# Graph attention and a routed FFN on one core: row fetches with a bound, and source numbers past it for rows of other destination blocks

## The chip, the cores and the metric

The kernel runs as one program on one core of a Trainium2 chip. The metric is the device time of one execution in microseconds (us); the figure given for a kernel is the median of its runs. The profile comes from one further execution; it counts times from the start of its own span. Engine names: PE is the matrix engine, PEld its weight load, DVE the vector engine, ACT the scalar engine, POOL the GpSimd engine, SP the engine that only issues DMAs. An engine's name with a q behind it (POOLq) is its instruction queue, that is, instructions which the sequencer carries out by itself.

## What is computed

There are 2500 nodes with 256 features and 80000 edges (`src`, `dst`), sorted by `dst`. The first half of the layer is a graph attention with 4 heads of 64 features; the second half is a feed-forward layer with 8 experts, of which each node takes two.

```python
h = einsum('nf,hfo->nho', layernorm(x), W)
e_s = einsum('nho,ho->nh', h, a_src)
e_d = einsum('nho,ho->nh', h, a_dst)
scores = leaky_relu(e_s[src] + e_d[dst], 0.2)
m = segment_max(scores, dst)
ex = exp(scores - m[dst])
alpha = ex / maximum(segment_sum(ex, dst)[dst], 1e-9)
agg = segment_sum(alpha[:, :, None] * h[src], dst)
x = x + relu(agg)
x = x + ffn(layernorm(x))    # 8 experts, top 2, HID = 512
```

## The kernel before

**Stages.** The program has three stages one after the other. The setup normalises `x`, multiplies it with the weights and stores one row per node in a DRAM table `h_tab` (2560 rows of 260 fp32: 256 of h, then e_s of the 4 heads). The edge loop fetches one such row per edge and sums them by destination. The last stage is the routed FFN.

**Tiles.** The nodes are cut into 20 blocks of 128 destinations (NB), the edges into 625 chunks of 128 (CHUNKS). A tile is one chunk seen by one block: where a block begins in the middle of a chunk, that chunk is in two tiles, once for either block. Each block has an even number of tiles, so some have a tile more than they need, and the program is built for the most that can be needed, NT = 664 tiles. For each tile a column of `srcP` holds the source numbers of its 128 edges, and a column of `Dcol` their destination less 128 times the block. An edge whose destination is in the block has a number from 0 to 127 there. Any other edge has one outside, its row of the one-hot matrix `dst_oh` is zero, and the row that was fetched for it adds nothing.

**Layout of the tiles.** DVE finds the counts (L985 to L1021). POOL fetches the chunks' edges by indirect DMA (L507) into `lay`; DVE makes `D_f` from the destinations (L1076), copies the sources to floats `s_f` (L1078), makes the marks between segments `RS_rows` (L1079 to L1082) and some flags, and tells the others by `lay_ready` (L1092). Then it zeroes `acc` (L1094). PE turns `D_f` and `s_f` (L604, first piece at the seventh of ten projections, which are L592), ACT copies them to `Dcol` and `srcP` (L793 to L800) and one small turned piece to `row_src` (L817), for which DVE waits at L1101.

**Edge loop.** It goes in phases of 32 tiles (PH) and in batches of 8 (BT). Whose turn it is:

- POOL issues one indirect DMA a tile (L529), 128 rows of 1040 bytes into the slot t mod 128 of `ring`. From tile 80 on (AHEAD) each eighth one waits until PE has done the batch 80 tiles back.
- DVE waits until a phase's 32 tiles have landed (`weights`, first instruction L1140), works out the maxima of the segments by scans, and multiplies the rows by the weights batch by batch (`weigh`, L1205, L1206). It adds PE's sums to `acc` (`flush`, L1118).
- ACT makes the one-hot matrices (L826, L831). PE multiplies them with the rows (`batch`, L641 to L643), two tiles to one sum.

**Order of the queues.** Each engine's order is written out by hand. Ahead of the first L529, POOL's queue holds 21 fetches of destinations (L496, L501), 6 of chunks (L507) and 20 scatters (L516), and waits for the stored `h_tab` and for the layout (L519 to L525). Behind the last one stand the FFN's gathers and scatters (L540, L549).

Of the kernel before, what the change touches and what calls it, by code (L numbers as in the profile page):

```python
# [37 lines left out]
def gat_moe_kernel(nc, x, src, dst, gnn_w, a_src, a_dst, gamma, beta, wr, br, w1, b1, w2, b2, out):  # L38
    fp32, bf16, i32 = mybir.dt.float32, mybir.dt.bfloat16, mybir.dt.int32
    ALU = mybir.AluOpType  # L40
    ACT = mybir.ActivationFunctionType
    AX = mybir.AxisListType
    P = 128

    N, F = x.shape
    H, _, FO = gnn_w.shape
    HF = H * FO
    KF = F // P
# [5 lines left out]
    NB = (N + P - 1) // P  # L55
# [6 lines left out]
    TG = (NPH * PH + P - 1) // P  # L62
# [9 lines left out]
    assert NT % BT == 0 and CHUNKS * P == E and RING % PH == 0 and H * PH == P  # L72
    MW = HF + H
    NE, _, HID = w1.shape
    FC = HID // P
    BS = 256
# [2 lines left out]
    NBLK = (TOP * N + NE * (BS - 1)) // BS  # L79
    EG = (N + BS - 1) // BS  # L80
    BIG = 1e38
    EPS = 1e-5

    h_tab = nc.dram_tensor("h_tab", (NB * P, MW), fp32).ap()
# [13 lines left out]
    with ctx:  # L98
        def sb(name, shape, dt=fp32):
            return ctx.enter_context(nc.sbuf_tensor(name, shape, dt))  # L100
# [12 lines left out]
        def early(width, dt=fp32):  # L113

            a = ring_flat[:, used[0]:used[0] + width]
            used[0] += width
            return a if dt == fp32 else a.bitcast(dt)
# [17 lines left out]
        D_f, s_f = (early(TG * P).rearrange("p (g e) -> p g e", g=TG) for _ in range(2))  # L135
        RS_rows = early(TG * P).rearrange("p (g e) -> p g e", g=TG)
# [23 lines left out]
        srcP = sb("srcP", [P, NPH * PH], i32)  # L160
# [320 lines left out]
        def _(pool):  # L481
# [8 lines left out]
            for t, pattern, mult in ((iota_f, [[1, P]], 0), (pcol, [[1, 1]], 1), (p128, [[1, 1]], P),  # L490
# [7 lines left out]
                in_offset=bass.IndirectOffsetOnAxis(ap=qbi[:, 0:1], axis=0)).then_inc(brow_in, 16)  # L498
            pool.wait_ge(q_ready, 1)
            for b in range(NB):  # L500
                pool.indirect_dma_start(  # L501
                    out=drow[:, b, :], out_offset=None, in_=dst_rows,
                    in_offset=bass.IndirectOffsetOnAxis(ap=qi[:, b:b + 1], axis=0)).then_inc(rows_got[b], 16)
            pool.wait_ge(chunks_ready, 1)
            pool.wait_ge(ds_put, 32)
            for g in range(TG):
                pool.indirect_dma_start(  # L507
                    out=lay[:, g, :], out_offset=None, in_=ds_tab,
                    in_offset=bass.IndirectOffsetOnAxis(ap=chunk_i[:, g:g + 1], axis=0)).then_inc(lay_in, 16)
# [16 lines left out]
            for t in range(NT):  # L526
                if t % BT == 0 and t >= AHEAD:
                    pool.wait_ge(batch_done, (t - AHEAD) // BT + 1)
                pool.indirect_dma_start(  # L529
                    out=ring[:, t % RING, :], out_offset=None, in_=h_tab,  # L530
                    in_offset=bass.IndirectOffsetOnAxis(ap=srcP[:, t:t + 1], axis=0))\
                    .then_inc(gathered[t // PH % len(gathered)], 16)

# [31 lines left out]
        def _(pe):  # L566
# [101 lines left out]
            def nodes_T(i):  # L668
                pe.wait_ge(x1_made, 1 + sum(2 * i + 2 > hi for _, hi in SETS))
                if i >= 2:  # L670
                    pe.wait_ge(xT1_copied, i - 1)
                for b in range(2):
                    for k in range(KF):
                        last = pe.transpose(bank[i % 2][:, (k * 2 + b) * P:(k * 2 + b + 1) * P],  # L674
                                            acc[:, 2 * i + b, k * P:(k + 1) * P], ident[:, :])
                last.then_inc(xT1_done, 1)
# [278 lines left out]
        def _(v):  # L955
            c = Chain(v, s_dve)
            v.memset(xs0[:, NB - 1, :], 0.0).then_inc(pads_set, 1)
            v.memset(bigs, -BIG).then_inc(bigs_set, 1)
            for t in (part_ends, C):
                v.memset(t[:, :], 0.0)  # L960
            v.memset(A_row[:, 0:1], -BIG)
            v.memset(D_row[:, P:P + 1], -BIG)
            v.memset(RS_all[:, :, P:P + 1], -BIG)
            v.wait_ge(ends_in, 16)
# [60 lines left out]
            def x_stats(lo, hi):  # L1025
# [9 lines left out]
                c.link(v.scalar_tensor_tensor(sm1[:, of], sm1[:, of], F / 4.0, sm2[:, of], ALU.mult, ALU.add))  # L1035
                v.tensor_scalar(sm1[:, of], sm1[:, of], 1.0 / F, EPS, ALU.mult, ALU.add).then_inc(var_ready, 1)

# [38 lines left out]
                last = v.tensor_scalar(D_f[:, g, :], lay_d[:, g, :], d_sub[:, g:g + 1], None, ALU.subtract)  # L1076
            c.link(last)
            v.tensor_copy(s_f, lay_s)  # L1078
            c.link(v.tensor_tensor(RS_rows[:, :, 1:P], D_f[:, :, 0:P - 1], D_f[:, :, 1:P], ALU.is_equal))  # L1079
            c.link(v.tensor_scalar(RS_rows[:, :, 1:P], RS_rows[:, :, 1:P], 1.0, BIG, ALU.subtract, ALU.mult))  # L1080

            v.memset(RS_rows[:, :, 0:P:PH], -BIG)  # L1082
            parts_of = D_f.rearrange("p g (i r) -> p g i r", r=PH)
# [192 lines left out]
            def stats(n):  # L1276
# [3 lines left out]
                for b in range(lo, hi):  # L1280
# [10 lines left out]

                v.tensor_scalar(tmp1[:, of], tmp1[:, of], (1.0 + EPS) / F, EPS * EPS, ALU.mult, ALU.add)\
                 .then_inc(var_ready, 1)
# [212 lines left out]
```

## Time and profile before

| | |
|---|---|
| time, median of 3 runs | 1388.14 us |
| lowest and highest of them | 1386.94 and 1390.61 us |
| span of the profiled execution | 1249.1 us |
| that execution's own time | not recorded beside its profile |
| first L529 starts, last L529 starts | 78.6 us, 910.4 us |
| POOL busy | 784.9 us (63%) |
| DVE busy | 726.1 us (58%) |
| PE busy | 661.5 us (53%) |
| ACT busy | 419.7 us (34%) |

The span begins with the first instruction and ends with the last. 1388.14 - 1249.1 = 139.0 us of a run's time lie around it, and no view shows them. POOL's busy time in a DMA row is the time in which it writes descriptors; the data move afterwards.

### The profile page before, as it was taken

The page shows a single profiled execution, that of the slowest core. Times are in us where ns is not written, and L with a number is a line of the kernel's source. Part 1 is how long each engine was busy: PE and PEld are TensorE (multiplying, and loading weights), DVE is VectorE, ACT ScalarE, POOL GpSimd, SP SyncE. Part 2 cuts the span into 40 slices and gives each one's busy share as a digit, 9 for nine tenths or more (in the row PEclk, how much of TensorE's full clock was granted, in tenths as well). Part 3 has the DMA queues.
Part 4 walks back from the last instruction along what each step waited for, and adds up shares of the span by engine and source line. Part 5 has one row for each costly group of instructions (what it writes and reads, how often), then busy time and mean ns, then how long its engine had stood idle before and what let it go on. Part 6 is the DMA issues. An engine that isn't in the chain of part 4 may idle for free.

```text
span 1249.1 us, 11021 instructions
## 1 busy us (share of the span) xinstructions
PE 661.5 (53%) x2666; PEld 524.6 (42%) x2666; DVE 726.1 (58%) x1781; ACT 419.7 (34%) x1058; POOL 784.9 (63%) x835
## 2 busy tenths in 40 slices
PE   0630343455335643465435643365447579999990
PEld 0520232244223432344324432244336558888880
DVE  6611476558665775558655775558677853333325
ACT  3550243144323443144423443144421532222210
POOL 5577777777777777777777777777710025555540
PEclk9975657787678766777677776776777579999995
DMA  8564434344444434444344444443491212222217
GB/s 281 177 119 108 110 106 109 109 111 110 107 110 110 110 107 108 109 111 110 107 111 110 111 107 109 109 111 106 118 357 44 84 34 69 76 72 72 68 59 254
DMA packets 79451, 143.95 MB, mean 115 GB/s; under 512 B 22337, under 2 KB 50467, under 8 KB 79267
## 3 DMA queue, kind: packets, MB, share of 16 engines
q0 software_dynamic: 39664, 110.31, 31.9%
q1 hardware_dynamic: 37147, 30.44, 8.0%
q10 hardware_dynamic: 2584, 2.56, 0.6%
q8 instruction: 22, 0.36, 0.1%
q14 instruction: 34, 0.28, 0.1%
HBM read 126.48 MB, written 17.40 MB: 115 GB/s over the span
## 4 chain that ended last, share of the span: by engine, by line
POOL 50%; PE 19%; issue 18%; DVE 6%; DMA 2%; PEld 1%; ACT 1%; PEldq 1%; DVEq 0%; POOLq 0%
POOL ring L529 49%; PE psum L731 7%; PE psum L745 7%; PE psum L592 1%; POOL ring L501 1%; PEld psum L641 1%; PEldq L643 1%; PE psum L719 1%; PE psum L683 1%; DVE acc L1479 1%; DVE acc L1480 1%; ACT ring L882 1%; PE psum L674 1%; DMA ring<-in_dst,ring 1%; DMA h_tab<-ring 1%
## 5 line engine op out<-in xcount | busy, mean ns | idle before, releaser
L529 POOL DMA_INDIRECT ring<-h_tab,srcP x664 | 630.8, 950 | 204.6 <-issue 201.9
L641 PE MATMUL psum<-ring,shared 128*128 128x260 f32 x1328 | 387.0, 448 | 450.5 <-DVE acc L1118 391.9
L641 PEld LDWEIGHTS psum<-ring,shared 128*128 128x128 f32 x1328 | 284.1, 222 | 540.2 <-DVE acc L1118 407.4
L826 ACT ACTIVATE shared<-iota_f,Dcol 128x128 f32<-128x128 f32 x664 | 202.0, 386 | 29.6 <-PEq L643 29.5
L1205 DVE TENSOR_TENSOR ring<-ring,psum 128x2048 f32<-128x2048 f32 x83 | 189.8, 2287 | 2.8
L844 ACT ACTIVATE Ex<-Z 128x128 f32<-128x128 f32 x21 | 6.5, 309 | 516.8 <-DVE Z L1172 516.8
L1118 DVE TENSOR_TENSOR acc<-acc,psum 128x260 f32 x332 | 140.0, 422 | 59.7 <-PEq L643 24.2
L1140 DVE STREAM_TRANSPOSE TB<-ring 128x128 f32<-128x128 f32 x21 | 8.5, 403 | 226.4 <-DMA ring<-h_tab,srcP 226.3
L540 POOL DMA_INDIRECT ring<-z_tab,ring x54 | 52.5, 972 | 116.4 <-DVEq L1418 100.3
L549 POOL DMA_INDIRECT ys_tab<-shared,ring x54 | 53.9, 998 | 85.5 <-DVE shared L1438 77.2
L928 ACT ACTIVATE RS_all<-psum,tail_consts 128x256 f32<-128x256 f32 x108 | 45.2, 470 | 158.0 <-PE psum L731 158.0
L745 PE MATMUL psum<-ring,RS_all 128*128 x432 | 97.5, 379 | 0.0
L731 PE MATMUL psum<-ring 128*128 128x256 f32 x432 | 97.5, 379 | 0.0
L831 ACT ACTIVATE shared<-shared,ones 128x1024 f32<-128x1024 f32 x83 | 95.3, 1149 | 2.7
L731 PEld LDWEIGHTS psum<-ring 128*128 128x128 f32 x432 | 82.0, 190 | 11.1
L745 PEld LDWEIGHTS psum<-ring,RS_all 128*128 128x128 f32 x432 | 80.1, 190 | 9.9
L1438 DVE TENSOR_TENSOR shared<-psum,links 128x512 f32<-128x512 f32 x27 | 18.7, 691 | 74.2 <-PE psum L745 74.2
L1430 DVE TENSOR_SCALAR ring<-psum,tail_consts 128x256 f32<-128x256 f32 x54 | 26.8, 538 | 53.0 <-PE psum L719 53.0
L516 POOL DMA_INDIRECT ed_tab<-e_node,spos x20 | 19.8, 991 | 12.9 <-ACT e_node L808 8.0
L1422 DVE COPY ring<-ring 128x1024 f32 x27 | 19.3, 713 | 14.0 <-issue 10.7
L501 POOL DMA_INDIRECT ring<-in_dst,ring x20 | 18.9, 946 | 10.5 <-issue 5.8
L592 PE MATMUL psum<-ring 128*128 128x264 f32 x80 | 20.3, 398 | 0.0
(293 smaller groups left out, 620.5 us busy)
## 6 DMA issues: line engine op xcount, KB each, us to landing
ring<-h_tab,srcP POOLq DMA_INDIRECT x664, 2.8
ring<-in_L_ffn_W SPq DMA_DIRECT2D x16, 512.0 KB, 11.0
h_tab<-ring SPq DMA_DIRECT2D x10, 260.0 KB, 2.6
ring<-in_x SPq DMA_DIRECT2D x1, 2432.0 KB
z_tab<-ring SPq DMA_DIRECT2D x2, 1024.0 KB, 4.4
ring<-ys_tab SPq DMA_DIRECT2D x4, 512.0 KB, 9.0
ring<-ys_tab ACTq DMA_DIRECT2D x4, 512.0 KB, 9.6
out<-acc SPq DMA_DIRECT2D x4, 512.0 KB
```

Of the source, the lines that this page charges most:

```text
L529: pool.indirect_dma_start(out=ring[:, t % RING, :], out_offset=None, in_=h_tab, in_offset=bass.IndirectOffsetOnAxis(ap=srcP[:, t:t + 1], a ...
L540: pool.indirect_dma_start(out=xs_in[:, u, m, :], out_offset=None, in_=z_tab, in_offset=bass.IndirectOffsetOnAxis(ap=node_ix[:, BM * j + m: ...
L549: pool.indirect_dma_start(out=ys_tab, out_offset=bass.IndirectOffsetOnAxis(ap=dest_ix[:, BM * j + m:BM * j + m + 1], axis=0), in_=y_out[:, ...
L592: last = pe.matmul(bank[2 + 2 * (i % 2) + b][:, 0:wide], xT0[:, i % 2, b, k, :], w_ext[:, k, :], start=(k == 0), stop=(k == KF - 1))
L641: pe.matmul(sums[G_at % NSUM][:, 0:MW], dst_oh[:, n % OHB, 2 * g + r, :], ring[:, t % RING, :], start=(r == 0), stop=(r == 1))
L731: last = pe.matmul(bank[2 + 2 * u + c // 2][:, c % 2 * BS:(c % 2 + 1) * BS], w1_now[:, u, k, c * P:(c + 1) * P], xsT[:, u, k, :], start=(k ...
L745: last = pe.matmul(bank[6 + u][:, m * F:(m + 1) * F], hT[:, u, c, m * P:(m + 1) * P], w2_all[:, bass.ds(e, 1), c, :].rearrange("p e f -> p ...
L826: last = act.activation(dst_oh[:, n % OHB, k, :], iota_f[:, :], ACT.Square, scale=-1.0, bias=Dcol[:, t:t + 1])
L831: act.activation(batch, batch, ACT.Relu, scale=-1.0, bias=ones[:, 0:1]).then_inc(oh_made, 1)
L928: act.activation(hT[:, u, c, :], bank[2 + 2 * u + c // 2][:, c % 2 * BS:(c % 2 + 1) * BS], ACT.Gelu, bias=b1_T[:, bass.ds(e * FC + c, 1)]) ...
L1118: v.tensor_tensor(a, a, sums[(n * GB + g) % NSUM][:, 0:MW], ALU.add).then_inc(flushed, 1)
L1205: v.tensor_tensor(msg, msg, ex.unsqueeze(3).broadcast_to([P, BT, H, FO]), ALU.mult)
```

## The change

A constant `FAR` (8192) is added. After the floats of the sources have been made, three DVE instructions on columns 1 to 5 of the six columns of tiles (each column has 128 tiles, so on tiles 128 to 767) work out D (D - 127), which is above 0 just where D is outside 0 to 127, make 8192 or 0 of it, and add that to the source number. They use `RS_rows`, which is written right after them, as their scratch. Each of the 664 fetches now has a bound, 2559, the last row of `h_tab`, and the mark that an index past the bound is no error: nothing is fetched for it. The slots of tiles from 128 on then keep the rows of the tile 128 before; the first 128 tiles fetch all their rows, since their slots hold something else before.

```diff
+    FAR = 8192
...
                 pool.indirect_dma_start(
                     out=ring[:, t % RING, :], out_offset=None, in_=h_tab,
-                    in_offset=bass.IndirectOffsetOnAxis(ap=srcP[:, t:t + 1], axis=0))\
+                    in_offset=bass.IndirectOffsetOnAxis(ap=srcP[:, t:t + 1], axis=0),
+                    bounds_check=NB * P - 1, oob_is_err=False)\
                     .then_inc(gathered[t // PH % len(gathered)], 16)
...
             v.tensor_copy(s_f, lay_s)
+            away = RS_rows[:, 1:TG, :]
+            far_of = D_f[:, 1:TG, :]
+            c.link(v.scalar_tensor_tensor(away, far_of, 1.0 - P, far_of, ALU.add, ALU.mult))
+            c.link(v.tensor_scalar(away, away, 0.5, float(FAR), ALU.is_gt, ALU.mult))
+            c.link(v.tensor_tensor(s_f[:, 1:TG, :], s_f[:, 1:TG, :], away, ALU.add))
             c.link(v.tensor_tensor(RS_rows[:, :, 1:P], D_f[:, :, 0:P - 1], D_f[:, :, 1:P], ALU.is_equal))
```

The order of DVE in the setup, before (all of these names lie in the buffer `ring`, which the setup uses as its scratch):

```order
L1076 TENSOR_SCALAR ring<-ring 128x128 x6
L1078 CAST ring<-ring 128x768
L1079 TENSOR_TENSOR ring<-ring 128x6x127
L1080 TENSOR_SCALAR ring<-ring 128x6x127
L1082 MEMSET ring 128x24
```

The same place with the change, where each line number is 2 to 7 higher:

```order
L1078 TENSOR_SCALAR ring<-ring 128x128 x6
L1080 CAST ring<-ring 128x768
L1083 SCALAR_TENSOR_TENSOR ring<-ring 128x640
L1084 TENSOR_SCALAR ring<-ring 128x640
L1085 TENSOR_TENSOR ring<-ring 128x640
L1086 TENSOR_TENSOR ring<-ring 128x6x127
```

Three instructions of 640 elements a partition have come in between the cast and the marks; nothing else has changed places on DVE, PE, ACT or SP. On POOL the 664 fetches stand where they stood.
How many rows are skipped follows from the inputs: 4352 of the 68608 rows of tiles 128 to 663 (6.3%). They are in 50 tiles, mostly in twos and threes at the border of two blocks; 18 tiles are skipped whole. Nine of these are the last nine, 655 to 663.

## Rows read from the trace of the kernel before

**Rows 1.** Busy time by stage: setup, edge loop, FFN (columns in the first line)
```profile
core 0: us, PE busy (x) PEld busy (x) DVE busy (x) ACT busy (x) POOL busy (x), PEclk, DMA share, GB/s
0.00:78.60 78.60, 28.32 (x145) 23.99 (x145) 43.79 (x139) 34.08 (x79) 47.71 (x63) 0.98 0.71 207
78.60:911.40 832.80, 371.96 (x1289) 275.14 (x1290) 520.34 (x1288) 303.91 (x791) 630.81 (x664) 0.71 0.41 111
911.40:1249.00 337.60, 261.18 (x1233) 225.46 (x1232) 161.96 (x355) 81.71 (x188) 106.41 (x108) 0.84 0.32 104
```

**Rows 2.** Groups of POOL: busy us, mean ns | idle before, releaser
```profile
L529 POOL DMA_INDIRECT ring<-h_tab,srcP x664 | 630.8, 950 | 204.6 <-issue 201.9 <-DMA h_tab<-ring 2.6
L549 POOL DMA_INDIRECT ys_tab<-shared,ring x54 | 53.9, 998 | 85.5 <-DVE shared L1438 77.2 <-issue 8.2
```

**Rows 3.** Line L529: duration in ns, least, median, most; who waited for it
```profile
L529 POOL DMA_INDIRECT ring<-h_tab,srcP x664: 942/946/1133, 78.6 to 910.4; - x166
...
  DVE TB L1140: 226.3, 20
...
DMA to landing us min/median/max: 2.7/2.8/3.9
```

**Rows 4.** Timeline around the end of the edge loop: POOL, then DVE
```profile
910.42 0.94 POOL L529 DMA_INDIRECT ring<-h_tab,srcP  x1 [0.30 <-issue]
...
924.72 0.40 DVE L1140 STREAM_TRANSPOSE TB<-ring 128x128 f32<-128x128 f32 x1
```

**Rows 5.** Other indirect DMAs, by line, as in Rows 3
```profile
L501 POOL DMA_INDIRECT ring<-in_dst,ring x20: 942/946/955, 11.1 to 34.8; - x20
...
L516 POOL DMA_INDIRECT ed_tab<-e_node,spos x20: 954/958/1148, 50.3 to 75.0; - x20
```

**Rows 6.** POOL's queue, lines L487, L505 and L523, as in Rows 3
```profile
L487 POOLq MOVE  x3: 29/29/35, 1.3 to 1.5; - x3
...
L505 POOLq EVENT_SEMAPHORE  x1: 17/17/17, 20.8 to 20.8; - x1
...
L523 POOLq EVENT_SEMAPHORE  x1: 43/43/43, 70.9 to 70.9; - x1
```

**Rows 7.** Timeline of POOL: start, us, what [idle before, releaser]
```profile
34.82 0.95 POOL L501 DMA_INDIRECT ring<-in_dst,ring  x1 [0.30 <-issue]
36.07 0.95 POOL L507 DMA_INDIRECT ring<-ds_tab,ring  x1 [0.30 <-issue]
...
53.17 1.15 POOL L516 DMA_INDIRECT ed_tab<-e_node,spos  x1 [0.30 <-issue]
54.62 1.15 POOL L516 DMA_INDIRECT ed_tab<-e_node,spos  x1 [0.30 <-issue]
56.07 0.96 POOL L516 DMA_INDIRECT ed_tab<-e_node,spos  x1 [0.30 <-issue]
...
75.01 0.95 POOL L516 DMA_INDIRECT ed_tab<-e_node,spos  x1 [0.31 <-issue]
78.60 0.99 POOL L529 DMA_INDIRECT ring<-h_tab,srcP  x1 [2.64 <-DMA h_tab<-ring]
```

**Rows 8.** Timeline of DVE in the setup
```profile
53.40 0.95 DVE L1079 TENSOR_TENSOR ring<-ring 128x762 f32<-128x762 f32 x1
54.38 0.56 DVE L1080 TENSOR_SCALAR ring<-ring 128x762 f32<-128x762 f32 x1
...
55.43 0.31 DVE L1091 COPY ring<-ring 128x6 f32<-128x6 f32 x1
...
64.68 0.17 DVE L1101 TENSOR_TENSOR ring<-psum,ring 128x6 f32<-128x6 f32 x1 [2.86 <-ACT ring L817]
```

**Rows 9.** Timeline of PE in the setup
```profile
62.46 0.60 PE L604 MATMUL psum<-ident,ring 128*128 128x128 f32 x4
```

**Rows 10.** DMA queue of POOL: packets, MB, share of 16 engines
```profile
q0 software_dynamic: 39664, 110.31, 31.9%
```

## Prediction

> **What bounds the kernel now.** I cut the span into its stages first [rows 1]: 78.6 us of setup, 832.8 us of edge loop, 337.6 us of FFN. In the edge loop no engine is busy all the time by that view; POOL has the most, 630.8 us of 832.8, and the DMA engines only 0.41 of theirs. The groups of POOL then show what fills the rest [rows 2]: 664 fetches of 950 ns on average and 201.9 us of idle time put down to "issue", which is time in which POOL waited for nobody. That is 201.9 / 663 = 0.305 us behind each. So POOL takes 950 + 305 = 1255 ns a tile without a break, and 664 x 1.255 = 833 us is the whole stage. The line's own view confirms it from the other side [rows 3]: the fetches are as good as equally long (median 946 ns), the wait for a batch that each eighth one carries has never held one up, and DVE waited 20 times, 226.3 us in all, for a phase to land. Everybody waits for POOL's descriptor writing. It is neither bytes nor DMA engines. A step in the edge loop is therefore worth what it does to those 1255 ns, and nothing else.
>
> One exception is at the end. The 21st phase starts on DVE at 924.72, and it did not wait for the fetches: the last had been issued at 910.42 + 0.94 and needs 2.8 us to land, so it was there at 914.2, 10.5 us early [rows 3, 4]. Phase 21 has the tiles 640 to 663. What changes in these 24 fetches is hidden by 10.5 us; what changes in the 640 before moves the end.
>
> **The change, part by part.**
>
> *Three DVE instructions in the setup.* The nearest rows have 762 elements and take 0.95 us (two inputs) and 0.56 us (one input) [rows 8]. For 640 elements that gives 0.80 + 0.47 + 0.80 = 2.1 us, between the cast and `lay_ready`, which comes at 55.7 now. Three wait behind them. PE's first turning of the layout starts at 62.46 [rows 9], 6.7 us after `lay_ready`, so it stays. DVE's L1101 waits 2.86 us for ACT [rows 8], which leaves 0.8. POOL's scatters beside DVE's work took 1.15 us and alone 0.96 [rows 7], so some two more scatters lie beside it and cost 2 x 0.19 = 0.4 us; the last of them ends at 75.96 and the first fetch waits until 78.60 for the stored table, so that is hidden by 2 us. All of it costs nothing. If the covers were gone it would be 2.1 us, once.
>
> *664 register moves.* A move on POOL's queue took 29 ns [rows 6]. One end of its price is that all is in series: 29 ns each, and 640 x 29 = 19 us. The other end is nothing, and three things speak for it. The wait of L505 stands behind the twentieth L501, which started at 34.82, yet it ran at 20.8, a dozen fetches ahead, and the gap at its place between L501 and L507 is 0.30 like every other [rows 6, 7]. L523 stands behind the last scatter (75.01) and ran at 70.9 [rows 6, 7]. The sequencer thus runs at least four DMAs ahead of the descriptor writing, and has 1255 ns per tile for a move of 29. I take nothing.
>
> *The bound in the fetch.* This is what decides, and the trace shows no fetch with a bound. The bounds of its price come from the other forms of the same instruction, all with 128 indices. L501 takes 946 ns at the median for rows of 2560 bytes, as L529 does for 1040, so bytes are free; L516, which writes by an index instead of reading by one, takes 958 [rows 3, 5]. The dearest form, L549, has a mean of 998, 48 ns above L529's 950 [rows 2]. A bound means that someone compares 128 numbers and treats some as absent, in every one of the 664, skipped rows or not. I take the step between the two nearest forms, 958 - 946 = 12 ns: 640 x 12 = 7.7 us. The ends are 0 and 640 x 48 = 31 us. Below nothing it can only come by what is skipped.
>
> *4352 rows less.* The DMA engines are at 0.41 and nobody waits for one for want of bandwidth [rows 1], so 6.3% fewer bytes bring nothing by themselves. A skipped row brings time only if POOL saves the writing of its descriptor. Split evenly, a row is worth at most 946 / 128 = 7.4 ns. Of the 4352 rows 9 x 128 = 1152 are in the covered phase 21, so at most 3200 x 7.4 = 24 us are there to have. The lower end is 0. I take 0, since that an instruction takes 942 to 946 ns whatever it moves [rows 3, 5] looks more like a fixed course than like work by the row; but all forms have 128 indices, so it does not exclude the other. The Trainium skill (DMA: Bandwidth & Descriptors, Anatomy of one DMA) calls descriptor generation "small, variable" and says that many descriptors can be emitted before the incremental cost shows. By that the saving would be 0 too, and a fetch here should be short; the row of 946 ns, which is not small, does not bear the first half out [rows 3].
>
> Sum: 0 + 0 + 7.7 - 0 = +7.7 us. The profiled execution's span becomes 1249.1 + 7.7 = 1256.8 us. With the 139.0 us around the span, which the change does not touch, the time is **1395.8 us**, 1388.14 + 7.7. The 139.0 come from the runs' median, as the profiled execution's own time is not given.
>
> **The rivals.** A measurement of this kernel can tell about 0.3% from no change, that is 4.2 us, or 6.5 ns on each of the 640 fetches. That is little.
>
> *A. Nothing happens.* The comparison fits into the fixed course, the moves hide: 1388 us. For it: 942, 946 and again 946 ns in quite different gathers [rows 3, 5]. Against it: a scatter, which differs by as little, is 12 ns longer.
>
> *B. Faster: skipped rows are not written.* It decides if POOL's time goes by the descriptors written and the test is cheap. With all of 7.4 ns a row it is -24 us, 1364 us; with half of it and no price for the test, 1376 us. It would need a saving of more than 12 x 640 / 3200 = 2.4 ns a skipped row to outweigh the price that I took. Against it: 4352 rows are few beside 664 instructions, so a price per instruction weighs 640 times and the saving sits in 41 tiles (the 50 less nine).
>
> *C. The moves are in series.* If a fetch that reads a register holds the queue until the one before is done, each tile has 29 ns more: +19 us, and with the forecast's 12 ns +26 us, 1414 us. Against it are the rows on L505 and L523; for it only that neither of them feeds the DMA behind it.
>
> *D. The test is made index by index.* Then it lengthens the writing by a share of 946 ns. A tenth gives 640 x 0.095 = 61 us and 1449 us, and there is no clear upper end. Against it: nothing in the rows shows a loop by the index. The Trainium skill (GPSIMD Engine Reference, Elementwise — side-by-side cycle accounting) states that data-dependent branching costs about 12 cycles an element on this engine; 128 of them at its 1.2 GHz would be an estimated 1.28 us a fetch and over 800 us in all, which would more than double the stage. No run here shows a branch by the element.
>
> **How the numbers follow.** Forecast (a few to 48 ns on each fetch, +4 to +31 us): 0.36. A, same: 0.34. B, faster: 0.17. C: 0.06. D: 0.07. So faster 0.17, same 0.34, slower 0.36 + 0.06 + 0.07 = 0.49. Cases of both signs have their part, but the forecast's own range is 1392 to 1419. The range for all goes down to 1368, which takes in most of B (its last 4 us need the full 7.4 ns a row), and up to 1425, which takes in the upper end of the forecast and C, and leaves out D. Some 0.07 + 0.04 + 0.03 are outside.
>
> **What would show it.** The fetch's own line shows nearly everything. Forecast: its median is 955 to 960 ns instead of 946, and the same in tiles with and without skipped rows, the gap behind it still 0.30, and the moves stand in POOL's queue well ahead of their fetches. A: median 946. B: the fetches of the 18 whole tiles, in pairs with their neighbours, are clearly shorter than 942, which now is the least. C: gaps of 0.33 or more. D: median above 1.0 us. In all cases the first fetch stays at 78.6 and `lay_ready` comes 2.1 us later; the bytes of the software queue fall by 4352 x 1040 = 4.5 MB from 110.31 [rows 10]. The prediction is wrong if the first fetch moves, if DVE no longer waits at L1140 (then another engine sets the pace, for which nothing speaks with DVE busy 520 of 833 us [rows 1]), or if fetches begin to wait for a batch.

## The result and the profile after

| | before | changed |
|---|---|---|
| median, lowest and highest of 4 runs | 1388.91 (1386.94 to 1390.61) us | 1397.30 (1395.32 to 1401.98) us |
| the profiled execution's own time | not recorded | 1395.32 us |
| its span | 1249.1 us | 1393.5 us |

The ratio is 1.0072, with a 95% interval of 1.0056 to 1.0088. The change costs 0.7%; the forecast was 1395.8 us.

The table's last two lines already break one step of the working. In the changed kernel the span falls short of the execution's time by 1.8 us, not by 139. No 139 us lie around a span. The profile of before was of another kind of execution than the runs beside it; with some 2 us around its span it took about 1251 us in all, an inference that the repeated runs below bear out. How that can be comes out in the experiments: **the same program took about 1390 us in the runs on some chips and about 1250 us in those on others.**

The stages of the changed kernel, in its own profile, to be held against [rows 1]:

```profile
core 0: us, PE busy (x) PEld busy (x) DVE busy (x) ACT busy (x) POOL busy (x), PEclk, DMA share, GB/s
0.00:86.40 86.40, 31.96 (x145) 26.39 (x145) 46.20 (x142) 34.63 (x79) 48.15 (x64) 0.96 0.63 189
86.40:1041.30 954.90, 407.55 (x1239) 307.35 (x1240) 510.62 (x1261) 291.00 (x756) 669.71 (x664) 0.69 0.34 91
1041.30:1393.50 352.20, 272.75 (x1284) 234.37 (x1282) 176.34 (x381) 95.94 (x224) 107.03 (x108) 0.85 0.32 104
```

The edge loop has grown from 832.8 to 954.9 us. Two costliest groups of its page, with the columns of [rows 2]:

```profile
L530 POOL DMA_INDIRECT ring<-h_tab,srcP x664 | 669.7, 1009 | 288.2 <-issue 188.7
L643 PE MATMUL psum<-ring,shared 128*128 128x260 f32 x1328 | 434.6, 495 | 488.6 <-issue 455.5
```

And the fetch's line, the counterpart of [rows 3]:

```profile
L530 POOLq MOVE  x664: 29/29/29, 85.6 to 1030.5; - x166
L530 POOL DMA_INDIRECT ring<-h_tab,srcP x664: 996/1002/1272, 86.4 to 1040.3; - x166
its engine sat idle before it (us, times) until:
  issue: 188.7, 618
  PEq L645: 96.5, 45
  DMA h_tab<-ring: 3.1, 1
who waited for it (us, times):
  DVE TB L1147: 30.2, 1
```

Two things differ from before, and only one of them is the change. A fetch takes 1002 ns at the median instead of 946. And POOL now waits for PE's `batch_done` (L645) 45 times, 96.5 us in all and 25 times for over 0.6 us, where in [rows 3] it never did, while DVE waits for a landed phase once instead of 20 times. The experiments first separate the two.

### The profile page after: what moved, and what is told of

Read it like the earlier page. It is cut to its first block, busy times and chain, and to the rows that moved or that the text cites. A ratio compares the mean times of both kernels' runs of the same rounds, so it can differ in the third digit from the quotient of the medians.

```text
span 1393.5 us, 11688 instructions
## 1 busy us (share of the span) xinstructions
PE 712.3 (51%) x2666; PEld 568.1 (41%) x2666; DVE 733.2 (53%) x1784; ACT 421.6 (30%) x1058; POOL 824.9 (59%) x835
## 4 chain that ended last, share of the span: by engine, by line
issue 38%; PE 17%; PEld 16%; DVE 12%; PEldq 9%; ACT 2%; DMA 1%; another core or an unknown queue 1%; POOL 1%; SPq 1%; DVEq 0%; POOLq 0%
PEld psum L643 16%; PEldq L645 8%; PE psum L733 7%; PE psum L747 6%; DVE acc L1125 2%; PE psum L594 1%; PE psum L721 1%; ACT ring L771 1%; PE psum L685 1%; DVE ring L1212 1%; DVE acc L1486 1%; POOL ring L502 1%; DVE acc L1487 1%; ACT ring L884 1%
## 5 line engine op out<-in xcount | busy, mean ns | idle before, releaser
L530 POOL DMA_INDIRECT ring<-h_tab,srcP x664 | 669.7, 1009 | 288.2 <-issue 188.7
L643 PE MATMUL psum<-ring,shared 128*128 128x260 f32 x1328 | 434.6, 495 | 488.6 <-issue 455.5
L643 PEld LDWEIGHTS psum<-ring,shared 128*128 128x128 f32 x1328 | 325.4, 252 | 586.6 <-issue 482.7
L551 POOL DMA_INDIRECT ys_tab<-shared,ring x54 | 54.4, 1007 | 85.0 <-DVE shared L1445 76.7
L632 PE MATMUL psum<-fm,oh_row 1*128 1x4 f32 x40 | 9.4, 302 | 66.6 <-issue 55.4
L632 PEld LDWEIGHTS psum<-fm,oh_row 1*128 1x128 f32 x40 | 8.1, 253 | 77.4 <-issue 65.9
L594 PE MATMUL psum<-ring 128*128 128x264 f32 x80 | 23.4, 443 | 3.8 <-issue 3.8
```

What stands on the lines that cost most here:

```text
L530: pool.indirect_dma_start(out=ring[:, t % RING, :], out_offset=None, in_=h_tab, in_offset=bass.IndirectOffsetOnAxis(ap=srcP[:, t:t + 1], a ...
L551: pool.indirect_dma_start(out=ys_tab, out_offset=bass.IndirectOffsetOnAxis(ap=dest_ix[:, BM * j + m:BM * j + m + 1], axis=0), in_=y_out[:, ...
L643: pe.matmul(sums[G_at % NSUM][:, 0:MW], dst_oh[:, n % OHB, 2 * g + r, :], ring[:, t % RING, :], start=(r == 0), stop=(r == 1))
```

## The experiments

They ran on four chips, one after another. The kernel before was timed beside them each time: 1395.08 us on the first, 1250.62, 1250.47 and 1252.72 us on the other three. Every ratio below is against the kernel before on the same chip.

### On a chip where before takes 1395 us

**The kernel before, again.** No edit.

> The kernel before, unchanged, profiled once more. Its page shows a span of 1249.1 us, its runs 1388 us, and the changed kernel's profile has 1393.5 us beside runs of 1397. Theory 1 (the 139 us lie around the span in every execution of before): span near 1249, time near 1388. Theory 2 (that profile caught an uncommon, undisturbed execution; an ordinary one has PE drains that go on long after the last matmul): span near 1387, several hundred us of PE idle put down to issue, DVE no longer waiting for the fetches, fetch median 946 ns.

Measured: 1395.26 us, ratio 0.9998 (0.9989 to 1.0007), span 1393.0 us. The fetch's line and PE's `batch_done` line of this run:

```profile
L529 POOL DMA_INDIRECT ring<-h_tab,srcP x664: 940/946/1161, 86.5 to 1033.9; - x166
its engine sat idle before it (us, times) until:
  issue: 190.7, 621
  PEq L643: 126.8, 42
...
who waited for it (us, times):
  DVE TB L1140: 28.4, 1
```

```profile
L643 PEldq DRAIN  x83: 1472/6965/35965, 151.7 to 1092.6; - x83
```

The kernel before has the waits for `batch_done` too, so they don't come from the change. Theory 1 falls: only 2.2 us lie around this span. Of theory 2 the long DRAINs hold, but the profile shown before was not an uncommon execution, as three more chips will show. The fetches are the 946 ns of [rows 3]. In the profile shown before, the same DRAIN reads so:

```profile
L643 PEldq DRAIN  x83: 1470/2785/6762, 132.0 to 948.6; - x83
```

Here it takes 6.97 us at the median instead of 2.79. The timeline of the repeated run shows what that looks like, PE first and then POOL:

```profile
308.89 3.77 PE L641 MATMUL psum<-ring,shared 128*128 128x260 f32 x16
...
325.27 1.20 PE L641 MATMUL psum<-ring,shared 128*128 128x260 f32 x2 [12.61 <-issue]
```

```profile
321.06 0.95 POOL L529 DMA_INDIRECT ring<-h_tab,srcP  x1 [0.30 <-issue]
325.32 0.94 POOL L529 DMA_INDIRECT ring<-h_tab,srcP  x1 [3.32 <-PEq L643]
```

PE's last matmul of the batch is over at 312.66, but the DRAIN behind it ends only at 325.1; from 313.1 DVE and ACT stand, and from 322.0 POOL too. POOL goes on 0.3 us after the DRAIN has ended. The trace has 44 such late ends among 83, each between 2.9 and 15 us after the last matmul and one 31 us after it; the other 39, and all 83 in the profile shown before, come within 0.03 us. POOL stops 41 times for over 0.6 us, mostly 16 tiles apart, 127.9 us in all. At 0.30 us each the same gaps would be 12.3 us, and the difference of 115.6 us is just what the time from the first to the last fetch has grown by (831.8 to 947.4 us). Ahead of it the span has 7.9 us more, behind it 20.4 us.

**The bound alone.** The added number is always 0, so no row is skipped; bound, register moves and the three instructions stay.

```diff
-            c.link(v.tensor_scalar(away, away, 0.5, float(FAR), ALU.is_gt, ALU.mult))
+            c.link(v.tensor_scalar(away, away, 0.5, 0.0, ALU.is_gt, ALU.mult))
```

> The change with 0 added in place of 8192, so that every row is fetched; bound and register moves stay, the three DVE instructions too. If the price is the bound in the instruction: fetch median 1002 ns as with the change, ratio 1.006 as the change. If the skipped rows cost or save: the ratio differs from the change's 1.0072 by more than 0.003, fetch median different from 1002 ns.

**The three instructions alone.** The same edit, and the fetch without `bounds_check`.

```diff
-                    bounds_check=NB * P - 1, oob_is_err=False)\
```

> The three DVE instructions alone, adding 0, with no bound and no moves. If they are covered as predicted: ratio 1.000 within 0.003, fetch median 946 ns. If the setup's DVE work carries the loss of 8 us: ratio 1.006 and the first fetch several us later than in before.

Measured: bound alone 1409.10 us, ratio 1.0107 (1.0091 to 1.0123); layout alone 1396.43 us, ratio 1.0010 (1.0001 to 1.0020). The two differ by the bound and nothing else, by 12.7 us. POOL's groups, the bound's first:

```profile
L530 POOL DMA_INDIRECT ring<-h_tab,srcP x664 | 669.0, 1007 | 294.6 <-issue 189.9 <-PEq L645 101.6 <-DMA h_tab<-ring 3.1
```

```profile
L530 POOL DMA_INDIRECT ring<-h_tab,srcP x664 | 631.4, 951 | 320.0 <-issue 188.9 <-PEq L644 127.9 <-DMA h_tab<-ring 3.2
```

The bound adds 669.0 - 631.4 = 37.6 us of descriptor writing, and 320.0 - 294.6 = 25.4 us less idle time stand against it, all of it from waits for `batch_done` (127.9 to 101.6). The rest is 12.2 us, close to the 12.7 measured. With the bound POOL stops 24 times for over 0.6 us, each time 24 tiles apart; without it 43 times, 8 or 16 tiles apart. The late ends are as many, 44 and 45, but with the bound 20 of the 44 find POOL not stopped. So on such a chip a slower POOL runs less often into a late signal, and two thirds of the bound's price are given back.

One more price is in these rows. ACT and POOL are let go by the same DRAIN; here is how they start, first in the repeated kernel before, then in the changed kernel:

```profile
325.09 2.44 ACT L826 ACTIVATE shared<-iota_f,Dcol 128x128 f32<-128x128 f32 x8 [13.04 <-PEq L643]
325.32 0.94 POOL L529 DMA_INDIRECT ring<-h_tab,srcP  x1 [3.32 <-PEq L643]
```

```profile
314.06 2.15 ACT L828 ACTIVATE shared<-iota_f,Dcol 128x128 f32<-128x128 f32 x7 [9.48 <-PEq L645]
314.79 1.00 POOL L530 DMA_INDIRECT ring<-h_tab,srcP  x1 [3.29 <-PEq L645]
```

POOL starts 0.23 us behind ACT without the bound and 0.73 us behind it with it. All stops of either trace are alike in this, so each of the 24 or 25 stops is 0.50 us longer, some 12 us in all. The fetch's move stands between the wait and the fetch there; whether it or the bound is the reason was not tried.

The layout's ratio has an interval that just leaves out 1: at most 0.2%, or 2.8 us.

**The kernel before, signal from the matmul.** The DRAIN is the instruction that carries `batch_done`. Is it the DRAIN that is slow?

```diff
-                        pe.matmul(sums[G_at % NSUM][:, 0:MW], dst_oh[:, n % OHB, 2 * g + r, :],
+                        last = pe.matmul(sums[G_at % NSUM][:, 0:MW], dst_oh[:, n % OHB, 2 * g + r, :],
...
-                pe.drain().then_inc(batch_done, 1)
+                last.then_inc(batch_done, 1)
```

> The kernel before, with batch_done told by each batch's last matmul in place of PE's drain. If the drain itself is what keeps PE in an ordinary execution after its last matmul: the time falls by over 100 us, to near 1250. If PE is held by something else (a matmul waits with it): no change within 1%, and the idle time of PE stays, in front of matmuls.

Measured: 1394.61 us, ratio 1.0004 (0.9989 to 1.0019). POOL's waits are still there, with a releaser that the trace can't name:

```profile
POOL ring L529 <- remote: 112.7, 27, 13.7
```

The columns are: time in total, number, longest. The late signal is not a matter of the DRAIN.

### On chips where before takes 1250 us

**The changed kernel, again.** No edit.

> The changed kernel, unchanged, on one chip with its parts. If skipping the rows gives something back: its ratio is below that of the bound alone (1.0107), near 1.007. If the difference between the two came from the chips: 1.010 to 1.011 here.

Measured: 1287.01 us against 1250.62, ratio 1.0300 (1.0286 to 1.0314); on the next chip once more, 1287.89 against 1250.47, ratio 1.0297 (1.0280 to 1.0314). The same change that costs 0.7% on the first kind of chip costs 3.0% here. The fetch's line:

```profile
L530 POOLq MOVE  x664: 29/29/29, 77.5 to 931.5; - x166
L530 POOL DMA_INDIRECT ring<-h_tab,srcP x664: 994/998/1204, 78.3 to 947.4; - x166
its engine sat idle before it (us, times) until:
  issue: 203.7, 664
who waited for it (us, times):
  DVE TB L1147: 262.4, 20
```

This is the profile that the forecast argued from, with the bound in it. POOL never waits, DVE waits 20 times, and the median has gone from 946 to 998 ns, 52 more. Over the 640 fetches that count, 640 x 0.052 = 33 us; by the busy sums, 668.0 - 630.8 = 37.2 us for all 664 (56 ns each at the mean), which is 35.9 us for 640. The gap is still 0.30 us. Fetch 640, counted from 0, starts at 917.29 against 881.45 before, 35.8 us later, the span grows by 35.8 and the time by 36.4. All of the loss is in the fetches' own duration.

The stage behind the last fetch, too, is as it was, 337.5 us against 337.6 in [rows 1]:

```profile
947.40:1284.90 337.50, 258.98 (x1234) 224.18 (x1234) 163.69 (x358) 83.06 (x190) 107.79 (x109) 0.85 0.32 104
```

What skipped rows are worth can be read from the fetches themselves. Five tiles in a row, number 532 to 536; the third has 38 rows skipped, the fourth all 128, the fifth 90:

```profile
775.74 1.00 POOL L530 DMA_INDIRECT ring<-h_tab,srcP  x1 [0.30 <-issue]
777.05 1.00 POOL L530 DMA_INDIRECT ring<-h_tab,srcP  x1 [0.31 <-issue]
778.35 1.00 POOL L530 DMA_INDIRECT ring<-h_tab,srcP  x1 [0.30 <-issue]
779.65 0.99 POOL L530 DMA_INDIRECT ring<-h_tab,srcP  x1 [0.30 <-issue]
780.95 1.00 POOL L530 DMA_INDIRECT ring<-h_tab,srcP  x1 [0.30 <-issue]
```

Over all tiles from 128 on, the median is 998 ns for the 486 that skip nothing, 998 for the 32 that skip some rows and 998 for the 18 that skip all. A skipped row saves nothing. That the rows are skipped is certain, since the software queue's bytes fell by 4.5 MB [rows 10], while the number of packets stayed:

```profile
q0 software_dynamic: 39664, 105.80, 30.0%
```

The sizes of these packets in the trace say what happens to such a row. Without skipped rows each packet of the fetches has 4160 bytes, four rows of 1040. With them 1075 packets have 16 bytes, and 26 have 3124, 2088 or 1052. That is just what comes out if 4352 pieces of 4 bytes stand where rows were. A skipped row is thus not left out, and it isn't true that nothing at all moves for it: a transfer of 4 bytes takes its place, and POOL's writing is as long as for a whole row.

**One register for all.** Is it the move ahead of each fetch?

```diff
+            last_row = pool.alloc_register("last_row")
+            pool.reg_mov(last_row, NB * P - 1)
             for t in range(NT):
...
-                    bounds_check=NB * P - 1, oob_is_err=False)\
+                    bounds_check=last_row, oob_is_err=False)\
```

> The changed kernel with the bound put into one register once, so that 663 of the 664 moves are gone. If the moves are hidden, as predicted: same ratio as the changed kernel within 0.002, fetch median 1002 ns, gap 0.30 us. If the moves carry the price: fetch and gap together fall towards 1251 ns a tile and the ratio towards 1.001.

Measured: 1288.37 us, ratio 1.0301 (1.0287 to 1.0315), the same as with 664 moves. The fetch keeps its duration:

```profile
L532 POOL DMA_INDIRECT ring<-h_tab,srcP x664: 994/998/1206, 79.4 to 948.8; - x166
```

On such a chip, where POOL never stands for a batch, the 663 moves cost nothing, and the whole price is in the instruction that has the bound. The bound and the mark `oob_is_err=False` were only run together.

**Half the rows.** The kernel before, but the first 320 fetches take 64 indices instead of 128, so half the edges of these tiles are left out. A POOL memset of the slots' other half stands once ahead of the loop (27.8 us).

```diff
-                    out=ring[:, t % RING, :], out_offset=None, in_=h_tab,
-                    in_offset=bass.IndirectOffsetOnAxis(ap=srcP[:, t:t + 1], axis=0))\
+                    out=ring[0:64 if t < 320 else P, t % RING, :], out_offset=None, in_=h_tab,
+                    in_offset=bass.IndirectOffsetOnAxis(ap=srcP[0:64 if t < 320 else P, t:t + 1], axis=0))\
```

> The kernel before, where the first 320 fetches have 64 indices and 64 partitions in place of 128 (the other half of each of these tiles is zeroed once and left out of the sums; one memset of POOL comes ahead of the loop). If the writing goes by the row: these fetches take near 473 ns, half of 946, and rows that are absent could have paid. If it is a fixed course: 900 ns or more. In either case the last 344 fetches take 946 ns.

Measured in one run: 1266.15 us, against 1252.72 for the kernel before. One fetch of 64 indices and one of 128, from the timeline of POOL:

```profile
300.60 0.90 POOL L531 DMA_INDIRECT ring<-h_tab,srcP  x1 [0.30 <-issue]
...
701.78 0.95 POOL L531 DMA_INDIRECT ring<-h_tab,srcP  x1 [0.30 <-issue]
```

Half the indices take 900 ns instead of 946 at the median, so an index that isn't there at all saves 46 / 64 = 0.72 ns. The time bears it out: the first fetch starts 28.1 us later, behind the memset, 320 x 0.046 = 14.7 us are won back, and 13.4 us are left, as measured. Had the skipped rows been left out of the list, 3200 x 0.72 = 2.3 us would have been there to have, a tenth of the 24 us that the prediction allowed. A tile skipped whole would then be some 92 ns shorter (an estimate, 128 x 0.72), and it isn't. If the step goes on in a straight line below 64, which no run shows, some 850 ns of the instruction do not depend on the number of rows (an estimate, 946 - 128 x 0.72). The Trainium skill (DMA: Bandwidth & Descriptors, Anatomy of one DMA) says of descriptor generation that many can be emitted before the incremental cost shows; with 0.72 ns a row this half of its statement agrees.

**POOL further ahead.** If POOL waits for `batch_done`, more room should help: the kernel before with `AHEAD = 112` instead of 80.

> The kernel before with AHEAD 112 in place of 80. In an ordinary execution POOL runs into its wait for batch_done and PE's long drains end 0.2 us before POOL goes on. If POOL really waits for work that is late, 32 tiles more of slack remove most of its waits and the time falls by 50 us or more. If PE's signals get through only once POOL is quiet, the same number of stops comes back 32 tiles later: time within 1%, some 40 stops, long drains as before.

Measured: 1250.54 us, ratio 1.0001 (0.9991 to 1.0010). On this chip POOL doesn't wait for `batch_done`, so the run says nothing on the other kind.

**Pauses of POOL.** The kernel before, where POOL waits at each 32nd tile until its own fetches have landed; in another kernel at each 24th.

```diff
             for t in range(NT):
+                if t and t % 32 == 0:
+                    f_was, in_f = (t - 1) // PH, (t - 1) % PH
+                    pool.wait_ge(gathered[f_was % len(gathered)], 16 * (PH * (f_was // len(gathered)) + in_f + 1))
```

> The kernel before, where POOL also waits at each 32nd tile until all its fetches have landed: 20 pauses of its own of some 2.8 us. If signals get through when POOL is quiet: these 20 pauses take the place of most of the 41 stops, and the time falls by up to (41 - 20) x 3.1 = 65 us, at least 20. If POOL's quiet has nothing to do with it: the pauses come on top, 20 x 2.8 = 56 us, or hide in slack, and the stops remain.

> The kernel before with a pause of POOL at each 32nd tile, once more, for a chip where before takes 1390 us (on one with 1250 it cost 2.75%). If the other engines' signals get through when POOL is quiet: the 20 pauses replace most of the 41 stops, and the ratio is under 0.985. If quiet has nothing to do with it: ratio 1.00 to 1.04. On a chip with 1250 us the run only repeats the 1.0275.

> The kernel before, with a pause of POOL until all has landed at each 24th tile: 27 pauses. On a chip where before takes 1250 us: the pauses come on top at the price of those at each 32nd tile (34 us / 20 = 1.7 us each), 27 x 1.7 = 46 us, ratio 1.037. On one where before takes 1390 us: if the others' signals get through when POOL is quiet, the 27 pauses replace the 41 stops, 14 x 2.5 = 35 us less, ratio 0.975; if not, ratio 1.00 to 1.05.

Measured: 1284.31 us, ratio 1.0275 (1.0259 to 1.0291), then 1284.73 us, ratio 1.0270 (1.0253 to 1.0287), and with each 24th tile 1299.23 us, ratio 1.0367 (1.0348 to 1.0385). Two lines from the views of POOL's waits, of 32 and of 24:

```profile
  DMA ring<-h_tab,srcP: 41.6, 20
```

```profile
POOL ring L532 <- DMA ring<-h_tab,srcP: 56.8, 27, 2.3
```

Each pause is 2.1 us, not the 2.8 that was expected, where the gap would have been 0.3: the 2.8 us of [rows 3] count from the start of a fetch, and 0.95 us of them are its own writing. The last pause of either run, at tile 640 or 648, has the slack at the end of the loop. The others make 19 x 1.8 = 34 us and 26 x 1.8 = 47 us; measured were 34 and 47. Every microsecond that POOL stands ahead of there is on the path here. The pauses were meant to show on the first kind of chip whether PE's late signals get through once POOL is quiet. None of them ran on such a chip, so that is **not tried**.

**The changed kernel, a third time,** with the result given above.

> The changed kernel a third time, to have it on the same chip as the next run. If this chip is one where before takes 1250 us: ratio 1.030, as POOL's 52 ns a fetch are all on the path. If it is one where before takes 1390 us: ratio 1.006 to 1.009, with POOL stopping each 24 tiles and not each 8 or 16.

No version beat the kernel before on either kind of chip; the best is the kernel before itself.

## Why the prediction was right and where it was not

The number was right within 1.5 us of 1397.3, and so was its direction, but the number by luck: two errors in it offset each other. What the working describes is the other kind of chip, and there its +7.7 us came out as +36.4. What follows goes by its steps.

*"The 139.0 us around the span."* This failed. It took a profile of one kind of execution and times of the other for one thing. The sum should have been made on 1249.1 + 1.8 = 1251 us, and the 139 us taken as a sign that the profile doesn't show what the runs did. A subtraction like this one needs an explanation before it may be carried along.

*POOL's 1255 ns a tile set the pace.* True in the profile shown and on three chips: the pauses were paid in full, and the bound too. Not true of the runs that were to be predicted. There POOL stands for 97 to 128 us in waits for `batch_done`, and added descriptor writing takes the place of a part of them. All three signs that the prediction named for being wrong are there (the first fetch at 86.4, one wait of DVE at the landing instead of 20, fetches that wait for a batch), but the repeated kernel before has them too, so none comes from the change.

*The three instructions, at nothing.* Right as far as can be told on the chips of 1250 us, where the first fetch starts at 78.26 to 79.42 with them, and at 78.37 to 79.91 in kernels without them. On the other 0 to 2.8 us, which a run doesn't separate from nothing with much certainty.

*The moves, at nothing.* Right on the chips of 1250 us, and shown by the single register. There the sequencer has run 12 fetches ahead, as the prediction had found at L505 (last move 931.5, last fetch 947.4). After a stop it has no such lead, and the 0.50 us that each stop is longer with move and bound, on the kind of chip that was timed, was in none of its terms.

*The bound, 12 ns between 0 and 48.* The mechanism was right, a fixed price in every fetch, skipped rows or not. The size was wrong: 52 ns at the median on one kind and 56 on the other, and 56 to 57 at the mean, in which the upper end of 48 was read. The term of 7.7 us was therefore 36 us, beyond its own end of 31. What misled was the choice of the nearest row: a scatter is as near as a gather of another form, but neither has a bound, and the price of a test that none of the rows contained can't be read from how they differ. The dearest form would have been the safer choice.

*4352 rows less, at nothing.* Right, against rival B. Tiles skipped whole take as long as others, and a skipped row still has a transfer of 4 bytes; even leaving indices out altogether brings 0.72 ns each.

*Only the first 640 fetches count.* Right: fetch 640 came 35.8 us later and the span grew by 35.8. The slack was read 1 us too short: 2.8 us from the start of the last fetch is 913.2, not 914.2, so phase 21 was there 11.5 us early. Nothing hangs on it.

So the 1395.8 came from two errors that offset each other. The bound was taken at a fifth of its price (7.7 for 36 us), and what the slower kind of execution gives back, 25 us in the comparison of bound and no bound on one chip, was not in the sum at all. On the chip of the result itself the changed kernel's profile is alone, since no profile of before exists there; that the same exchange happened there is inferred from its 96.5 us of waits beside its 669.7 of fetches. Why the bound alone cost 1.07% and the whole change 0.72%, in another session, wasn't settled; the session, perhaps the chip, and the skipped rows all differ. The fetches are as long in both (1007 and 1009 ns). Of the 13.0 us between the two spans 0.6 lie ahead of the first fetch, 5.6 in the loop and 6.8 behind the last fetch.

Of the rivals, A (nothing happens) falls with the 52 ns, C (moves in series) with the single register and the gap of 0.30, and D (index by index) as it was priced: its tenth of 946 ns would be 95 ns. Its sign, a median above 1.0 us, was badly placed, since 1002 ns meet it and 998 don't. And 52 ns for 128 indices are also 0.4 ns an index; whether the test is made once or per index was not tried, since no fetch with a bound and fewer indices was run.

## What to carry to other kernels

First hold the profiled execution's own time against the runs; if they differ by a tenth, the profile shows another behaviour than the one that is timed, and no term may be taken from it without asking which. In a loop that one engine's descriptor writing paces, an option of the DMA instruction is paid at every issue: here the bound cost 5.5% of each of 664 fetches, and what it skipped, 6% of the rows, had never been what anyone waited for. Where descriptor writing is the limit, skipped rows bring nothing; fewer fetches should, but none of the runs had fewer.

## What the runs showed of the hardware

- **Two kinds of chip.** Unchanged, the kernel took 1388.9 and 1395.1 us in two groups of runs and 1250.5 to 1252.7 us on three other chips, each time within 0.4% on the one chip. Each chip was seen once, and that of the first group isn't on record, so it isn't shown that the chip, and not the hour or what else ran beside it, makes the kind. The mean granted clock was 0.749 in the repeated kernel on the first kind and 0.764 in the profile shown before; 2% don't account for ends that come 3 to 15 us after the last matmul is over.
- **Where it goes.** On the slower kind, the sequencer of PE finds its batch finished late in 44 of 83 batches, all but once 3 to 15 us after the last matmul has ended (312.66 to 325.1 in the rows above). In the repeated kernel before, 41 of the 44 ends fall in POOL's stops, mostly 1.3 to 4.3 us after its last descriptor writing. That suggests that signals get through when POOL is quiet, but the changed kernel's own profile doesn't bear it out: 19 of its 44 late ends come while POOL fetches without a stop. One of them, at 517.4, 7 us after the last matmul:

```profile
506.70 3.75 PE L643 MATMUL psum<-ring,shared 128*128 128x260 f32 x16 [0.23 <-issue]
...
516.72 1.00 POOL L530 DMA_INDIRECT ring<-h_tab,srcP  x1 [0.30 <-issue]
517.57 1.56 DVE L1125 TENSOR_TENSOR acc<-acc,psum 128x260 f32 x3 [3.91 <-PEq L645]
...
518.02 1.00 POOL L530 DMA_INDIRECT ring<-h_tab,srcP  x1 [0.30 <-issue]
```

  What makes the ends late stays open. In the traces of this kind most records of the fetches' semaphores are missing too (1781 are left of 10623 in the repeated kernel before), so that the view of the fetches has no time of landing.
- **The price list of an indirect DMA on POOL** with 128 indices: 946 ns, with a bound 998 or 1002, with 64 indices 900, and 0.30 us between two of them in each case. A row skipped by the bound costs the same writing as a row fetched, and moves 4 bytes.
